# Moving the experts ahead of the output projection in the last two full stages, and the transposes of an expert sum between the next tile's experts

## The reference

```python
x = x + attn_block(layernorm(x))
    # xn = ln(q_x)*w+b; q,k,v = xn@w; fq, fk = elu(.)+1
    # kv = einsum('bhnd,bhne->bnde', fk, v)      (per token, over the 16 heads)
    # attn = fq@kv / (fq.ksum + 1e-6); x1 = q_x + attn@wo + bo
    # x1 + gelu(ln(x1)@fc_w + fc_b) @ proj_w + proj_b
z = layernorm(x)
pooled = z.mean(axis=1)                           # per sequence
gates = softmax over the top 2 of (pooled @ gate_w.T + gate_b)
x = x + sum over e of gates[e] * gelu(z @ expert_w[e].T + expert_b[e])
```

## Time and profile before

| | us |
|---|---|
| median of 3 runs | 1216.74 (1216.59 to 1218.15) |
| the profiled execution, its own time | 1216.43 |
| its span, first to last instruction | 1214.6 |
| TensorE busy | 1066.1 (88%) |
| VectorE busy | 791.8 (65%) |
| ScalarE busy | 528.7 (44%) |
| mean granted TensorE clock | 0.912 |

### The profile page before, as it was taken

How to read it: one execution, slowest core, us unless ns; L and a number is a source line. 1 busy time by engine, 2 the same in 40 slices (tenths; PEclk the granted TensorE clock), 3 DMA queues, 4 the chain that set the end, 5 groups by cost and what they waited for, 6 DMA issues and landing times.

```text
span 1214.6 us, 21887 instructions
## 1 busy us (share of the span) xinstructions
PE 1066.1 (88%) x7112; PEld 789.0 (65%) x7112; DVE 791.8 (65%) x1756; ACT 528.7 (44%) x835; POOL 184.0 (15%) x113
## 2 busy tenths in 40 slices
PE   5646988979798989999998899999999899796856
PEld 3334767767685858686776758686867667584623
DVE  2466576767666677768776676867687675656333
ACT  2414353635444443636364344636363444232322
POOL 1001111112111011211121111212112111202000
PEclk9858898979797989999997999999999899898969
DMA  4896948585857758676766658686767586321023
GB/s 169 172 189 135 170 105 174 109 176 107 173 112 160 146 127 181 150 171 142 178 132 169 138 131 174 146 183 147 172 139 177 130 174 140 84 56 62 21 76 108
DMA packets 331610, 170.23 MB, mean 140 GB/s; under 512 B 292752, under 2 KB 309392, under 8 KB 331280
## 3 DMA queue, kind: packets, MB, share of 16 engines
q1 hardware_dynamic: 324880, 158.81, 60.5%
q10 hardware_dynamic: 6656, 10.50, 2.5%
HBM read 93.75 MB, written 75.50 MB: 139 GB/s over the span
## 4 chain that ended last, share of the span: by engine, by line
PE 70%; issue 13%; DVE 9%; ACT 3%; POOL 2%; DMA 2%; SPq 0%; ACTq 0%; DVEq 0%; POOLq 0%
PE pq L980 15%; PE pj L966 13%; PE ps L943 10%; PE pq L888 9%; PE pt L952 5%; PE pq L925 4%; PE ps L925 3%; PE ps L1023 3%; PE pt L925 3%; PE pj L1069 2%; DVE am L705 2%; PE pt L876 2%; DVE acc L836 1%; DVE nd L737 1%; POOL x_sb L458 1%
## 5 line engine op out<-in xcount | busy, mean ns | idle before, releaser
L721 DVE TENSOR_TENSOR hidden<-xhT,hidden 128x512 fp32r<-128x512 f32 x128 | 88.5, 691 | 222.0 <-ACT hidden L546 221.4
L545 ACT ACTIVATE xhT<-pq,col 128x512 f32<-128x512 f32 x128 | 88.0, 688 | 324.5 <-PE pq L980 324.3
L980 PE MATMUL pq<-hT,w_fc 128*128 128x512 f32 x768 | 220.9, 426 | 4.8 <-issue 3.0
L966 PE MATMUL pj<-w_pj,hidden 128*128 128x256 f32 x1536 | 214.3, 289 | 2.7 <-DVE hidden L721 2.7
L966 PEld LDWEIGHTS pj<-w_pj,hidden 128*128 128x128 f32 x1536 | 191.6, 189 | 17.3 <-DVE hidden L721 3.7
L943 PE MATMUL ps<-kq 48*128 48x128 f32 x1024 | 155.3, 434 | 34.1 <-DVE am L705 19.7
L943 PEld LDWEIGHTS ps<-kq 48*128 48x128 f32 x1024 | 133.9, 330 | 75.1 <-issue 44.1
L705 DVE TENSOR_TENSOR am<-ps,mask 128x512 f32<-128x512 f32 x256 | 164.3, 683 | 26.1 <-PE ps L943 25.3
L980 PEld LDWEIGHTS pq<-hT,w_fc 128*128 128x128 f32 x768 | 147.3, 205 | 35.5 <-issue 4.7
L888 PE MATMUL pq<-zT,w_e 128*128 (+1 forms) x256 | 115.4, 604 | 7.9 <-DMA b_e<-in_eb 7.4
L552 ACT ACTIVATE ot<-pt,den_eps 128x512 f32<-128x512 f32 x64 | 78.9, 1233 | 31.6 <-PE pt L952 31.6
(11 more groups left out here) (114 smaller groups left out, 1298.4 us busy)
## 6 DMA issues: line engine op xcount, KB each, us to landing
kq<-scratch_q SPq DMA_DIRECT2D x192, 128.0 KB, 3.6
kq<-scratch_k SPq DMA_DIRECT2D x192, 128.0 KB, 4.5
scratch_q<-hidden SPq DMA_DIRECT2D x32, 512.0 KB, 4.6
scratch_k<-hidden SPq DMA_DIRECT2D x32, 512.0 KB, 6.1
scratch_nd<-ot SPq DMA_DIRECT2D x32, 512.0 KB, 4.4
nd<-scratch_nd SPq DMA_DIRECT2D x96, 128.0 KB, 2.6
x_sb<-in_x SPq DMA_DIRECT2D x16, 512.0 KB, 4.7
scratch_v<-feat_v ACTq DMA_DIRECT2D x16, 512.0 KB, 2.8
```

Of the source, the lines that this page charges most:

```text
L545: nc.scalar.activation(gelub[:, u], pq[u][:, :], ACT.Gelu, bias=b_fc[:, m:m + 1])
L721: nc.vector.tensor_tensor(hidden[:, m % SLOTS, 1], gelub[:, u], hidden[:, m % SLOTS, 0].bitcast(f32), ALU.subtract).then_inc(S["rest_ready ...
L966: last = nc.tensor.matmul(pj[u][:, D * s:D * (s + 1)], hidden[:, m % SLOTS, a, lo:lo + P], w_pj[:, b, m], start=(m == 0 and n == 0 and s = ...
L980: last = nc.tensor.matmul(pq[m % 2][:, :], w_fc[:, b, c, P * m:P * (m + 1)], hT[:, a, c], start=(n == 0), stop=(n == len(order) - 1))
```

## The change

Three edits, all in the last stages. In stages 16 and 17 a list written out by hand puts `F1, F3, F4` ahead of `A2` and `R` (and `SA` ahead of `B0`). The transposes, add and store of an expert sum become a stage `F9` with lag 8, which in stages 20 to 22 runs for the tile before, between `F1` and `F3`; stage 19 loses its `F2`, and a last `F9` follows behind the loop. In the loop `XL` stands behind `F9`. Since `acc` is one buffer, `F1` on VectorE waits in the loop until the transposes of the tile before have read it.

```diff
+       "H": 2, "J7": 3, "JA": 3, "XS": 4, "J2": 4, "Z": 4, "E": 4, "F1": 7, "F3": 7, "F4": 7, "FX": 7, "XL": 7, "F2": 7, "F9": 8}
...
-            run(Place(s, i, base, rates))
+            run(Place(s, i, base, rates, "F1" in names and "F9" in names))
...
-    stages(without(FULL, *first), 16, [])
-    stages(without(FULL, *first, *second), 17, [])
+    ends = ["XS", "M1", "VL", "K0", "J2", "Y", "M2", "M3", "Z", "M4", "N0", "XL", "J7", "JA", "YB", "E", "VT", "N", "K1",
+            "F1", "F3", "F4", "A2", "R", "SA", "B0", "H", "FX", "B9", "F2"]
+    stages(ends, 16, [])
+    stages(without(ends, *second), 17, [])
     stages(["XS", "C1", "J2", "C2", "Z", "C3", "C4", "XL", "J7", "JA", "E", "F1", "F3", "F4", "FX", "F2"], 18, [])
-    stages(["XS", "J2", "Z", "XL", "E", "G", "F1", "F3", "F4", "FX", "F2"], 19, [])
-    loop(20, 23, last)
+    stages(["XS", "J2", "Z", "XL", "E", "G", "F1", "F3", "F4", "FX"], 19, [])
+    loop(20, 23, ["F1", "F9", "XL", "F3", "F4", "FX"])
+    stages(["F9"], 23, [])
...
                 if p.stage == "F1":
                     wait("gate_ready", at("gate_ready"))
+                    if p.overlapped:
+                        for u in range(2):
+                            wait(f"pj_full{u}", at(f"pj_full{u}", 1))
...
-                if p.stage == "F2":
-                    wait("acc_ready", at("acc_ready"))
+                if p.stage in ("F2", "F9"):
+                    wait("acc_ready", at("acc_ready", -NC if p.overlapped else 0))
```

More of the change, by code:

```diff
@@ L46 @@
 LAG = {"L": 0, "DS": 0, "D1": 0, "X": 0, "D2": 0, "K0": 1, "K1": 1, "VL": 1, "VT": 1, "B0": 1, "B9": 1, "Y": 2, "N": 2, "A2": 2, "R": 2, "YB": 2, "SA": 2, "N0": 2,
-       "H": 2, "J7": 3, "JA": 3, "XS": 4, "J2": 4, "Z": 4, "E": 4, "F1": 7, "F3": 7, "F4": 7, "FX": 7, "XL": 7, "F2": 7}
+       "H": 2, "J7": 3, "JA": 3, "XS": 4, "J2": 4, "Z": 4, "E": 4, "F1": 7, "F3": 7, "F4": 7, "FX": 7, "XL": 7, "F2": 7, "F9": 8}
 FULL = ["L", "XS", "M1", "VL", "K0", "J2", "Y", "M2", "DS", "M3", "Z", "D1", "M4", "N0", "XL", "X", "J7", "JA", "YB", "E", "VT", "N", "D2", "K1", "A2",
@@ L87 @@
     "ps_free1": {"B0": 1, "B9": 1, "D2": 1, "A2": 1, "E": 1, **rounds("ps_free1")},
-    "pj_full0": {"J7": 1, "F2": 1}, "pj_free0": {"JA": 1, "F2": 1}, "pj_full1": {"J7": 1, "F2": 1}, "pj_free1": {"JA": 1, "F2": 1},
+    "pj_full0": {"J7": 1, "F2": 1, "F9": 1}, "pj_free0": {"JA": 1, "F2": 1, "F9": 1}, "pj_full1": {"J7": 1, "F2": 1, "F9": 1}, "pj_free1": {"JA": 1, "F2": 1, "F9": 1},
     "x_in": {"L": 16},
@@ L103 @@
     "acc_ready": {"P": 1, "F1": 2, "F4": 2},
-    "out_stored": {"P": 16, "F2": 16},
+    "out_stored": {"P": 16, "F2": 16, "F9": 16},
     "dve_chain": {"N0": 2, "N": 3, "DS": 2, "A2": 2, "J2": 2, "G": 13},
@@ L114, with __init__ @@
 class Place:
-    def __init__(self, stage, i, base, rates):
+    def __init__(self, stage, i, base, rates, overlapped):
         self.stage, self.i, self.base, self.rates = stage, i, base, rates
         self.t = i - LAG[stage] if stage in LAG else None
+        self.overlapped = overlapped
     def at(self, name, more=0):
```

## The result

The changed kernel took 1209.13 us in the median of 5 runs (1207.90 to 1211.79), the kernel before 1216.74. The ratio is 0.9936, with a 95% interval from 0.9922 to 0.9950.

What follows compares the result with a forecast made beforehand. TensorE, 70% of the chain, was taken as the bound, with waits in stages 16, 17 and the last tiles. Terms -1.3 - 0.5 - 2.1 = -3.9 us took the median 1216.74 to 1212.8 us, range 1209.2 to 1215.4.

Steps and rivals of the forecast that it cites:

- The experts run in the wait, and A2 runs at full clock: Stages 16 and 17: expert matmuls fit TensorE's waits of 7.74 and 8.64 us; A2 then takes about 3.2 us.
- A2 to H, 9.1 us in stage 16 and 8.9 in 17: Time from A2's start to H's transposes, predicted to start at 1046.9 us in stage 16 and 1110.4 in 17.
- VectorE's four operations are hidden: Stage 16: 2.5 us of expert work on VectorE lies beside A2, without delaying A2's adds.
- The clock falls behind A2 and is at 0.50 from H on: Stages 16 and 17: TensorE drops to half clock before H's transposes; dense matmuls then stay at half clock 3.8 us.
- Its price: Half clock's cost: stage 16 gains 1.3 us (3.3 at full clock), stage 17 gains 0.5 (3.1 at full clock).
- H, B9 and F2 at half clock: Stage 16: three small TensorE groups take 1.85, 2.3 and 1.85 us, from 1046.9 to 1052.9.
- B9's 2.3, which no row shows, is doubled: Stage 16: B9's score matmuls assumed to take 2.3 us at half clock, or 1.2 if weight loads set their time.
- + 0.3: Stage 16: loss from half clock lasting 0.5 us longer once stage 17's dense matmuls begin; half of that is lost.
- The tail: Last tiles: add, store and load through one buffer set rounds of 7.95 us; the last add comes 2.1 us earlier.
- the tail by TensorE: Rival for the last tiles: transfers don't bind, TensorE sets the period of 7.81 us; 1209.3 us, chance 0.05.
- the clock that holds: Rival for stages 16 and 17: TensorE stays at full clock; 8.5 us gained in all, 1208.2 us, chance 0.07.
- the transfers: Rival for the last tiles: slower add, store, load rounds turn the end slower, 1222.4 us with 11.15 us rounds; chance 0.06.

Runs made afterwards that it cites:

- e11: Changed kernel, but in stages 16 and 17 VectorE alone runs its four F1 and F4 operations behind A2's adds and statistics; 1211.96 us.
- e5: The changed kernel measured again with its code unchanged, in another job; 1211.30 us, ratio 0.9957 to the kernel before.
- e4: Changed kernel plus matmuls that nothing reads on TensorE between A2 and H in stages 16 and 17; 1204.95 us.
- e3: Changed kernel, but the last four tiles use buffers of their own, the free slots of x_sb; 1208.51 us.
- e6: As e3, but each tile's x2 load is issued ahead of the store of the tile before; 1208.42 us.

## Why the prediction was right or wrong

- *The experts run in the wait, and A2 runs at full clock:* right, in both stages.
- *A2 to H, 9.1 us in stage 16 and 8.9 in 17:* 8.54 and 8.53. The second add started 3.1 us behind A2's start, not 3.36, and POOL's power took 1.02, not 1.20. That is 0.5 and 0.4 us of gain that the sum didn't have.
- *VectorE's four operations are hidden:* right, shown by e11, where the second add starts no earlier without them.
- *The clock falls behind A2 and is at 0.50 from H on:* right in both stages.
- *Its price:* wrong, and this is the step that failed. "H, B9 and F2 at half clock" was 6.0 us and measured 4.67, because "B9's 2.3, which no row shows, is doubled" was false: the score matmuls took 1.2 us at either clock. The other end of the bound, 1.2, was right. This one term is 1.1 us, and with it alone the sum would have been -5.0. The trace of the kernel before had a row for it that the prediction missed (below). F2's transposes took 1.6 us to the next start, not 1.85. The "+ 0.3" in stage 16's sum, for a longer half clock once stage 17's matmuls begin, was 0: from the first L980 to the next E it is 37.3 us before and after. In stage 17, H to U was 3.48 (3.8 predicted), and from the first L980 to the first L966 half clock cost 1.07, not 1.5. Stage 16 gave 3.4 us in place of 1.3, stage 17 1.6 in place of 0.5.
- *The tail:* right in its mechanism, that the chain of transfers would be the bound and that the first add comes 3 us later against the experts. The round was 8.17 us in place of 7.95, 1.56 from add to store issue (1.44 predicted), 3.23 to the load's issue (3.16) and 3.38 for load and wake (3.35); three rounds make the tail 1.6 in place of 2.1.
- *The sum:* 3.9 predicted, 6.7 by the stretches. By the stretches the time would be 1216.74 - 6.7 = 1210.0 us, inside the range, so that the first measurement fell just below it is chance; that the gain was put too low is not. The remaining 0.9 of the first measurement lies ahead of stage 16. That it is unrelated rests on the same code starting stage 16 two microseconds later in e5. The granted clock has a part in it: of 73 executions of the kernel before in four jobs, the four with a mean clock of 0.918 to 0.922 took 1209.16 to 1211.42 us and all others, at 0.905 to 0.914, 1214.22 to 1222.26. What decides the clock in one execution is open. Stages 16 and 17 gave 3.2 us more than the sum had, up to the gate: 1.1 are B9, 0.9 the earlier H, 0.7 the half clock once dense matmuls began, 0.5 the rest of H to U. The tail took 0.5 back.
- *The rivals:* none of them came, though the first measurement, 1209.13, lies next to the times of two (1209.3 for the tail by TensorE, 1208.2 for the clock that holds). The clock did not hold, the transfers did not take more than they gave, and the tail did not go by TensorE.

B9's price at half clock, in the first 100 us of the kernel before (timeline, then window, columns as in rows 5):

```profile
82.27 1.23 PE L943 MATMUL ps<-kq 48*128 48x128 f32 x8
```

```profile
82.27:83.40 1.13, 1.13 (x12) 1.04 (x8) 0.00 (x0) 1.00 (x1) 0.00 (x0) 0.50 0.65 161
```

## What to carry to other kernels

Work that sits behind a late operand in an in-order queue is worth moving ahead of it even if it was covering something else: ask what the idle engine will cost as well (here the half clock that followed took back 4.6 us of 9.6), and price half clock per instruction, from rows at half clock: the score matmuls didn't slow down, the transposes nearly doubled. A loop that is freed from one wait falls to the next chain: load, add and store through one buffer were 1.8 us of slack before and 5 us of waiting after, and a second buffer shortens the tail fully only once the load also leaves the queue behind the store. Look at what the earlier load then runs beside: here it held up the experts' weights by 0.8 us of the 1.1 it had gained. Where parts of a program vary by more than the effect, compare stretches between marks of the trace and not whole times.

## What the runs showed of the hardware that was not expected

- Eight score matmuls (48-row weights, 128 columns) took 1.23 us at a granted clock of 0.50 and 1.21 at 1.00, eight transposes 1.97 and 1.04 to 1.10. The eight weight loads of the score matmuls took 1.04 us together at either clock, those of eight transposes 1.57 and 0.86; that the weight loads set the pace of the score matmuls is likely from that, but not tested.
- POOL's power of 128x4 took 1.20 us when VectorE worked beside it (before, e11) and 1.02 when VectorE stood idle (after, and e4, where TensorE worked beside it).
- Two 256 KB loads of expert weights took 2.3 us to land (median) by themselves (e3) and 3.4 beside a 512 KB load (e6).
- The same instructions ahead of stage 16 took from 1027.05 to 1033.94 us in traces of kernels that share that code.
